# Normalised rows moved from VectorE to GpSimd, statistics and the load of x moved one slot ahead

## The reference

```python
h = jnp.maximum(_layernorm(x, axis=-1), 0.0)
x = x + _L0_gnn_ref(h, adj, ...)

# inside _L0_gnn_ref, called with x = h
xc = jnp.transpose(x, (0, 2, 1))
h = relu(_bn(_conv1d(xc, conv1_w, 0), ...))          # 1x1 convolution
h = _bn(_conv1d(h, conv2_w, 8), ...)                 # 17 taps
x_conv = jnp.transpose(jax.nn.relu(h + xc), (0, 2, 1))
# then distances, masked messages, a GRU cell; layer 1 follows
```

## Time and profile before

| | |
|---|---|
| Time, median of 3 runs | 1869.83 us (1867.81 to 1880.15) |
| The profiled execution's own time | 1870.98 us |
| Its span, first to last instruction | 1868.8 us |
| TensorE busy in the span | 1768.8 us (95%) |
| VectorE busy | 1495.5 us (80%) |
| ScalarE busy | 875.8 us (47%) |
| GpSimd busy | 439.2 us (24%) |
| The 66 slots of the convolution stage | about 78 to 400 us |

### The profile page before, as it was taken

One profiled execution on the slowest core, in us unless ns is written; L12 is line 12 of the kernel. 1 busy time (PEld: TensorE's weight loads), 2 busy tenths in 40 slices (PEclk: granted clock), 3 DMA queues, 4 the chain that ended last, 5 costly groups with the idle time before them and its releaser, 6 DMA issues.

```text
span 1868.8 us, 36896 instructions
## 1 busy us (share of the span) xinstructions
PE 1768.8 (95%) x12477; PEld 1167.3 (62%) x12478; DVE 1495.5 (80%) x3322; ACT 875.8 (47%) x1617; POOL 439.2 (24%) x616
## 2 busy tenths in 40 slices
PE   3768999999998999999999999999999999999996
PEld 1456777764445666666666666666666666666664
DVE  4899999962346888888888888888888888888886
ACT  3675555553344444444444444444444444444442
POOL 4511111101012222222222222222222232222221
PEclk9899999999999999999999999999999999999999
DMA  6298887767732322322322322322322322322320
GB/s 201 98 331 261 303 295 270 265 224 250 253 132 94 104 76 81 102 78 80 101 79 80 100 80 79 100 81 78 99 83 76 99 84 75 100 85 74 101 86 17
DMA packets 175187, 245.56 MB, mean 131 GB/s; under 512 B 14781, under 2 KB 111028, under 8 KB 174635
## 3 DMA queue, kind: packets, MB, share of 16 engines
q1 hardware_dynamic: 175128, 244.81, 39.9%
HBM read 154.57 MB, written 90.18 MB: 131 GB/s over the span
## 4 chain that ended last, share of the span: by engine, by line
PE 40%; DVE 21%; ACT 5%; issue 3%; DVEq 0%; POOL 0%; POOLq 0%
PE ps_rz L1551 18%; PE ps_l L1551 13%; PE ps_n L1551 7%; ACT big L1696 3%; ACT big L1591 3%; DVE big L1687 2%; DVE big L1586 2%; DVE big L1621 2%; DVE big L1643 2%; DVE big L1595 2%; DVE big L1578 2%; DVE big L1730 2%; DVE big L1704 2%; PE ps_d L1765 2%; DVE big L1734 2%
## 5 line engine op out<-in xcount | busy, mean ns | idle before, releaser
L1551 PE MATMUL ps_rz<-big 128*128 128x512 f16 x2304 | 560.6, 379 | 13.0 <-DVE big L1643 10.7
L1551 PEld LDWEIGHTS ps_rz<-big 128*128 128x128 f16 x2304 | 220.0, 98 | 224.0 <-DVE big L1643 20.0
L1551 PE MATMUL ps_n<-big 128*128 128x256 f16 x2304 | 314.2, 273 | 0.0
L1551 PEld LDWEIGHTS ps_n<-big 128*128 128x128 f16 x2304 | 225.3, 98 | 94.5
L1551 PE MATMUL ps_l<-big 128*128 128x512 f16 (+1 forms) x1536 | 271.9, 327 | 2.9 <-DVE big L1800 1.5
L1264 PE MATMUL m_ps<-big 128*128 128x512 f16 (+1 forms) x1152 | 268.3, 375 | 3.0 <-DVE big L1029 2.2
L1721 POOL TENSOR_TENSOR big<-big 128x256 f32<-128x256 f32 x128 | 97.5, 762 | 666.9 <-ACT big L1714 666.9
L1696 ACT ACTIVATE big<-big,w_scale 128x512 f32<-128x512 f32 x128 | 92.0, 719 | 283.3 <-DVE big L1687 283.3
L1551 PEld LDWEIGHTS ps_l<-big 128*128 128x128 f16 x1536 | 149.9, 98 | 90.9 <-DVE big L1800 2.0
L1551 PE MATMUL ps_b<-big 128*128 128x256 f16 x1536 | 188.6, 272 | 1.5 <-DVE big L1621 1.5
L1264 PEld LDWEIGHTS m_ps<-big 128*128 128x128 f16 x1152 | 111.8, 98 | 105.1 <-issue 2.2
(11 more groups left out here) (242 smaller groups left out, 2892.7 us busy)
## 6 DMA issues: line engine op xcount, KB each, us to landing
spectra<-ysb SPq DMA_DIRECT2D x96, 256.0 KB, 2.4
big<-spectra SPq DMA_DIRECT2D x64, 384.0 KB, 3.5
xin<-in_x SPq DMA_DIRECT2D x64, 256.0 KB, 4.0
x_normed<-front SPq DMA_DIRECT2D x64, 256.0 KB, 4.3
h_turned<-front SPq DMA_DIRECT2D x64, 256.0 KB, 3.9
big<-h_turned SPq DMA_DIRECT2D x64, 256.0 KB, 3.2
big<-in_adj SPq DMA_DIRECT2D x64, 256.0 KB, 3.6
big<-in_x SPq DMA_DIRECT2D x64, 256.0 KB, 2.8
```

The lines of the kernel that those rows point to most:

```text
L1551: last = pe.matmul(dest, stationary(dl), moving(wl), start=start and n == 0, stop=stop and n == 2, **kw)
```

## The change

The rows of `normalise` are now written by GpSimd, directly behind the `rstd` of the same graph, with the same two waits for the buffer (the transposes of graph `f - 2`, and the landed store of graph `f - 2`). VectorE takes statistics one slot earlier (of graph `q + 2` in slot `q`) and waits in addition until the rows of the graph two before have been normalised, since its `meanvar` is read by GpSimd. SyncE loads x of graph `q + 3` in slot `q` instead of `q + 2`; one more load stands ahead of the loop. The waits inside `load_x`, `store_xhat` and `store_h` are as they were.

```diff
@@ SyncE
+                load_x(2)
                 for q in range(SLOTS):
-                    if q + 2 < graphs:
-                        load_x(q + 2)
+                    if q + 3 < graphs:
+                        load_x(q + 3)
                     if q < graphs:
                         load_adj(q)
@@ GpSimd
-                layer_rstd(0)
-                for q in range(graphs - 1):
-                    layer_rstd(q + 1)
+                def normalise(f):
+                    pool.wait_ge(rstd_done, f + 1)
+                    if f >= 2:
+                        pool.wait_ge(turned, f - 1)
+                        pool.wait_ge(xhat_stored[f % 2], 16 * (f // 2))
+                    for t in range(H):
+                        last = pool.tensor_scalar(xhat[:, f % 2, t, :], xin[:, f % 2, t, :], meanvar[:, f % 2, t, 0:1],
+                                                  rstd[:, f % 2, t:t + 1], ALU.subtract, ALU.mult)
+                    last.then_inc(xhat_done, 1)
+
+                for f in range(graphs):
+                    layer_rstd(f)
+                    normalise(f)
@@ VectorE
                 def layer_stats(f):
                     dve.wait_ge(x_loaded[f % 2], 16 * (f // 2 + 1))
+                    if f >= 2:
+                        dve.wait_ge(xhat_done, f - 1)
...
-                def normalise(f):
...
                 layer_stats(0)
-                normalise(0)
+                layer_stats(1)
                 for q in range(SLOTS):
-                    if q + 1 < graphs:
-                        layer_stats(q + 1)
+                    if q + 2 < graphs:
+                        layer_stats(q + 2)
                     if q < graphs:
                         split_h(q)
...
-                    if q + 1 < graphs:
-                        normalise(q + 1)
```

## The result

| | before | after |
|---|---|---|
| median of the runs, us | 1869.30 (1867.81 to 1880.15) | 2055.72 (2052.77 to 2062.22) |
| profiled execution, its own time and span, us | 1871.0, 1868.8 | 2052.77, 2050.9 |
| TensorE's mean granted clock, 1 being 2.4 GHz | 0.992 | 0.958 |

What follows compares the result with a forecast made beforehand. SyncE's one-slot store loop was taken to bind: 85.2 us, then 12 x 8.34 + 49 x 6.85 = 435.8, put the last transposes at 526.0 instead of 386.9. That 139 us on 1871.0 gave 2010 us, range 1960 to 2086.

Steps and rivals of the forecast that it cites:

- SyncE's order is the term that decides: In SyncE's queue, the store behind the waiting load of x closes a one-slot loop; it had two slots, 9.9 us.
- Rival 1: On SyncE's queue, the store doesn't lie behind the load's wait, so the loop is hidden: 1867 us, no change; 6%.
- middle slots: Convolution slots after the filters, bound by VectorE: 4.43 to 3.70 us without its rows, 4.2 us for six slots.
- The loop's length: Convolution stage, rows to next rows through SyncE's store: 6.85 us without filters, 8.34 us in twelve slots with them.
- The rows: Two row instructions per graph on GpSimd: 1.05 us each, 2.1 us a pair; bounds 1.85 and near 3.3.
- My bound of 2.44 for a pair: GpSimd's row pair at twice the longest one-operation instruction; with 4.0 us to landing, the sum is 2051 us.
- the port's worst case, 42 us: GpSimd's rows and VectorE's lower half of h1 excluding each other wholly: 0.69 x 61 = 42 us more.
- the 1.3 that the prediction names as a sign of being wrong: On GpSimd, a row instruction under 0.9 or over 1.3 us would show the forecast wrong.
- the 1926 us worked out from it: End of the sum if GpSimd's rows took 0.77 us a pair, by the skill's best case; not taken.
- The store: SyncE's store of the rows, issue to landing: 3.6 us without filters, 4.7 with, plus 0.08 to GpSimd's start.
- rival 2: TensorE's clock stays at half speed past slot 18, 9.9 us a slot: 146 us more, 2156 us; 3%.
- What would show it: Signs across engines: GpSimd waiting some 3.5 us a slot, TensorE 1.9, rstd 6.9 and 8.3 us apart, DMA share two thirds.

Runs made afterwards that it cites:

- three_x: Changed kernel with three buffers for x instead of two, SyncE's queue order as changed: 1877.91 us, ratio 1.0031.
- store_first: Changed kernel with SyncE's store of the rows of graph q moved ahead of the load of x of graph q+3: 1886.38 us, ratio 1.0085.
- three_rows: Changed kernel with three buffers for the normalised rows instead of two, queue order as changed: 1876.49 us, ratio 1.0036.
- load_only: Kernel before, rows still on VectorE, with only SyncE's load of x made one graph further ahead: 1927.71 us, ratio 1.0314.
- one_operand: Changed kernel with VectorE's lower half of h1 reading its first operand from PSUM instead of SBUF, without the bias: 2041.3 us, ratio 1.0913.
- covered: three_x with VectorE's statistics moved from the slot's head to between the bias sum and the lower half of h1: 1877.22 us, ratio 1.004.
- adj_last: Changed kernel with adjacency load and filter store moved behind the store of the rows, load of x still ahead: 1966.2 us, ratio 1.0513.
- best: covered with the store of the rows ahead of the load of x, and graph 0's rows on VectorE: 1870.57 us, ratio 1.0003.
- best_padded: best with two tiny memsets added on GpSimd ahead of the rows: 1870.59 us, ratio 1.0005.

## Why the prediction was right in sign and 46 us short

**SyncE's order is the term that decides: right.** The loop shows in the timeline, and breaking it at any place takes the loss away: at the load's wait (three_x), at the order (store_first), at the buffer (three_rows). load_only has it without GpSimd. Rival 1 is refuted by the slots, and its 1867 us also by its own term, see the middle slots below.

**The loop's length: the row pair was mis-sized.** Taken 6.85 and 8.34 us; the changed kernel has, in the mean of the 12 loops with filters and of the 49 later ones:

| step | filters: taken, measured | later: taken, measured |
|---|---|---|
| rows, a pair | 2.10, 2.74 | 2.10, 2.69 |
| wait and issues to the store | 1.46, 1.47 | 1.07, 0.98 |
| store's issue to the next rows | 4.78, 4.57 | 3.68, 4.01 |
| loop | 8.34, 8.77 | 6.85, 7.68 |

By these, the sum's own way: the rows of graph 1 end at 81.76 us (85.2 taken: the stage's first statistics start at 73.54 us against 77.92 before; what comes ahead of them is not part of the change, and in the five experiments that leave the start of the stage as changed the first row instruction comes 0.6 to 3.7 us later than here), twelve loops add 5.2 us to what I took, the 49 others 40.8, and the last step from the rows of graph 62 to the last transposes is 5.05 where I had 5.0. -3.4 + 5.2 + 40.8 = 42.6: the last transposes at 568.63 instead of 526.0. That is the profiled execution, 2052.8 us; the median lies 2.9 us above it.

- *The rows*, 61 x 0.60 = 37 us of it. I took 1.05 us an instruction, between the one-operation row at 0.92 and twice that the earlier trace rows. It is 1.22 without neighbours (one_operand), so 0.33 a pair or 20 us are the operation's own price; 0.27 a pair or 16 us are the port. My bound of 2.44 for a pair, from a disturbed instruction with one operation, met the undisturbed value of 2.43 by luck; the port's worst case, 42 us, stood beside it and was left out of the sum. With the port the mean instruction took 1.35 us, over the 1.3 that the prediction names as a sign of being wrong. The Trainium skill ("GPSIMD Engine Reference", 3.1) gives 769 ns for 512 elements in the best case; half of that, 0.38 us, is an estimate from its figure that lies further off still, and so does the 1926 us worked out from it.
- *The store*, 49 x 0.33 = 16 us, less 12 x 0.21 = 2.5 us in the filters' slots. Past them its usual value is near what I took (median 3.65 against 3.68); the mean lies above since some land late, of which more below. I had reasoned from a median where a loop pays the mean.
- *The issues*, 0.09 less each, -4 us.

**Port contention.** The timeline above shows it both ways. At 402.30 VectorE's instruction begins just before the second row instruction would, and keeps its 0.69 us; the pair takes 2.96 instead of 2.43. At 409.98 the second row instruction has been under way for 0.12 us; the pair keeps 2.43 and VectorE's takes 0.97. The Trainium skill ("SBUF — State Buffer", "SBUF: two separate sides") says that whoever starts first gets the shared pair of ports for the whole instruction and that the other fully blocks. That one of the two waits, this trace bears out. "For the whole instruction" it doesn't: VectorE's instruction ended at 410.95, before the row instruction did at 411.07. And where VectorE's began 0.43 us or more into the second row instruction, nine times in this trace, neither took longer, as here:

```profile
238.36 2.43 POOL L831 TENSOR_SCALAR front<-xin,meanvar,rstd 128x256 f32<-128x256 f32 x2 [3.60 <-DMA x_normed<-front]
240.07 0.69 DVE L1025 SCALAR_TENSOR_TENSOR front<-c,front 128x512 f16<-128x512 f32 x1 [0.62 <-ACT front L915]
```

Only a VectorE instruction that was running when a row instruction began, or that began at most 0.26 us behind it, cost either of them something. Nor do the recorded starts always tell who pays: at 478.20 VectorE's began 0.14 us behind the first row instruction, and it was the pair that took longer, 2.97 us. The measured 14.4 us are a third of the 42 that this rule's worst case gave, for two reasons: 40 of the 61 pairs took longer at all, and these by 0.41 us in the mean and 0.54 at most instead of 0.69.

**Middle slots: wrong step.** "There a slot falls from 4.43 to 4.43 - 0.73 = 3.70 us on VectorE" counted the removed instructions as removed time. They had covered a wait of 0.63 us for ScalarE, as three_x shows (4.43) and covered confirms (3.84). For rival 1's 1867 us the 4.2 us were thus not to be had by this change, loop or no loop. It did not touch the forecast, since the loop binds those slots too.

**TensorE's clock, rival 2: refuted as a price, but not for the reason given.** I held a fall unlikely since TensorE would be busier than in a stretch that had the full clock. The clock did fall, to 0.66 from 300 to 310 us, and to 0.83 from 340 to 380, where TensorE was busy 30.28 of 40 us. Half speed throughout, as the rival has it, did not come: from 240 us on, stretches of 20 us lie between 0.80 and 1.00. And TensorE is not in the loop: GpSimd's rows waited for the store and the load of x for the rows, sixty-one times each, and neither ever for TensorE; the loops are accounted for without it.

**What would show it.** GpSimd's wait: 257.7 / 61 = 4.2 us a loop, "some 3.5" said (the late stores and the filter slots are in it). TensorE's wait at the transposes: 148.9 / 58 = 2.6 us, 1.9 said, for longer slots. DMA share 0.78 to 0.54, about two thirds. Third stage unchanged: 1475.15 us after the last bias sum, 1474.8 before. First rstd instructions 8.8 and 7.5 (median) to 7.7 us (mean) apart, 8.3 and 6.9 said.

## What to carry to other kernels

Before moving a wait in a queue that is issued in order, list what stands behind it: if the waiting transfer needs this graph's work and the transfer behind it frees the buffer of the next, two buffers do the work of one, and the slot becomes wait, issues, flight and compute in a row. Put the transfer that frees a buffer ahead of the one that fills one, or give either one more buffer; each took away nine tenths of the loss here. And before crediting an engine with the instructions that are taken from it, look at what it waits for right behind them.

## What was not expected of the hardware

**Late stores beside an instruction fetch.** Of the 61 stores of rows in the changed kernel, 16 had an instruction fetch of 16 KB in flight, and from issue to the next rows 15 of these took 4.4 us or more, typically 5. Of the 39 without any fetch most took 3.5 to 3.7, the ones at 4.1 to 4.5 mostly in the filters' slots, and none longer; the other six had a fetch of 8 KB and took 3.6 to 4.9. One of the former, the DMA queues from 248.2 to 254.8 us (packets, MB, share; then the issue, KB, us to landing):

```profile
q8 instruction: 1, 0.02, 0.9%
...
x_normed<-front SPq DMA_DIRECT2D x1, 256.0 KB, 5.3
```

From 209.8 to 214.9 us, without one, it was 3.5 us. This is a correlation; no run took the fetches away. A fetch alone doesn't make a store late, either: in adj_last, where only the load of x lies just ahead of the store, 14 of the 61 had a fetch of 16 KB in flight, and ten of them took 3.2 to 3.7 us. What else it takes stays open.

**Transfers ahead of the store.** Past the filters, from the store's issue to the next rows took a mean of 3.56 us with only x just ahead (adj_last) and 4.01 with x and the adjacency; the medians are 3.48 and 3.65, so most of the mean's difference is in the late ones.

**The speed of a later stage.** The same code took 20.05 us a graph in twelve of the fourteen kernels here, before and after among them, and 20.05 and 20.26 by turns, 20.15 in the mean, in `best` and `best_padded`; not explained.
